# Norm statistics per batch and weight splitting per piece, inside the causal and the merged stage

## The chip, the cores and the metric

The kernel runs on one core of a Trainium2 chip. The metric is the device time of one execution in microseconds (us), the median of several runs. A core has a matmul engine (PE, its weight loads shown apart as PEld), a vector engine (DVE), an activation engine (ACT), a general engine (POOL) and a sync engine (SP) that here only issues DMAs. Each engine runs its own instructions in order, and the engines meet by semaphores.

## The reference, cut to what matters

Two layers follow each other on 16 batches of 256 rows with 256 features. The context has 77 rows per batch.

```
h = layernorm(x + multihead(x, x, x, sa_w..., causal=True))            # 16 heads of 16
h = layernorm(h + multihead(h, ctx, ctx, ca_w..., causal=False))
x = layernorm(h + relu(h @ ff_w1.T + b1) @ ff_w2.T + b2)              # hidden size 1024
q, k, v = x @ Wq + bq, ctx @ Wk + bk, ctx @ Wv + bv                    # second layer, one head
a = softmax(q k^T / 16) v
out = a * mask * sigmoid(concat(q, a) @ Wg + bg) + x

layernorm: std = sqrt(sum((x - mean)^2) / (d - 1));  gamma * (x - mean) / (std + 1e-6) + beta
```

## The kernel before, in words

Everything is fp32 accuracy made from products of two or three parts: a matrix is split in a high part (a rounded copy, made on ACT) and a low part (the rest, made on DVE or POOL), and three matmuls replace one (helper `mm3`, line 76).

The program is a row of stages. Between two stages all engines meet at a barrier (`Sems.stage`):

1. `context_products`: keys, values and folded weights that depend on the context alone, written to DRAM.
2. `self_attention`, here called the causal stage: causal attention, residual into `t.res` (all 16 batches stay in SBUF), and per 128 rows `bn_stats`/`bn_aggr` into `t.mv` (mean and variance).
3. `finish_stats`: for all 32 row groups at once `std = Sqrt(var)` on ACT, then `mean`, `rstd` on DVE.
4. `split_weights`: loads ca_wq, ca_wo, ff_w1, ff_w2 through two staging buffers and splits each in two.
5. `cross_feed_forward`, here called the merged stage: the first norm applied, cross attention, a second norm, feed-forward, statistics of the third.
6. `finish_stats` again.
7. `gated_attention`, the gated stage: third norm applied, second layer, output.

Stages 2 and 5 are software pipelines written out by hand. A list `slots` runs over pairs (n, s). The causal stage has U = 12 slots per n, the merged stage U = 8. Each engine walks the same list and does, in each slot, what its own loop says, for batches n-4 to n+4. So a batch is many slots under way, and in a steady batch period each engine does one batch's worth of every step. Names used later:

- Causal stage. PE: `scores_turned(g)` writes transposed scores to one of two buffers `a_st`, and waits for the exponential of two units before. `project_qk` (slots 3 to 6), `project_v` (slots 9, 10; it waits for `s_r1`). ACT: `exps(g)` one unit per slot (`a_pT<-a_st`), then in slot 7 `part_one` (`a_parts<-a_misc`). DVE: `remainder` (`a_rest`) makes `s_r1`. `moments` in slots 3 and 4.
- Merged stage. PE: one buffer `c_st` for transposed scores; `up_tile` and `down_tile` of the feed-forward, one each per slot. ACT per slot: `exps`, `hidden_high` (`c_hh`). In slot 6 of every batch there is already a `deviation`: the standard deviation of the second norm as exp(0.5 ln(var)), two activations on 2 columns. DVE follows in slot 7 with `inverse`: reciprocal, times var, plus std, scale, reciprocal (one refinement step of the root), each waiting for the one before.
- `feed_residual`, `feed_moments`: residual and statistics for the third norm, for batch n-6 or n-7.
- SP in the merged stage, per batch in this order: `store_parts`, `load_keys` (6 DMAs), `load_values`, `load_queries` (3 DMAs, after the store has landed).
- First in the merged stage DVE clears two tiles `c_nm` and sets rows of three `c_sk` to one, and waits for all of them.

## Time and profile before

| | us |
|---|---|
| runs shown | 1029.33, 1028.06, 1033.78 |
| median | 1029.33 |
| profiled execution, its own time | 1023.21 |
| its span, first to last instruction | 1021.5 |
| PE busy | 835.2 (82%) |
| DVE busy | 634.9 (62%) |
| ACT busy | 481.3 (47%) |
| POOL busy | 465.0 (46%) |
| mean granted clock of PE | 0.895 of full |

Start and end of the stages in the profiled execution, read from the timeline: context stage to 80, causal stage to 422, statistics and weights to 443, merged stage to 898, statistics to 902, gated stage to the end. Busy time is summed over stages that have different limits. A row of the timeline gives start, duration, engine, line, output<-inputs, a count of merged instructions, and in brackets how long the engine had stood idle and what released it.

### The profile page before, as it was taken

How to read it: one execution, taken by the hardware profiler on the slowest of the kernel's cores; microseconds unless marked ns; L12 is line 12 of the kernel's file. 1: busy time of each engine (PE TensorE's matmuls, PEld its weight loads, DVE VectorE, ACT ScalarE, POOL GpSimd, SP SyncE). 2: the span in 40 equal slices, each digit the busy share in tenths (PEclk: the TensorE clock that was granted, in tenths of full speed). 3: DMA queues.
4: the chain of work that ended last, by engine and by line, in shares of the span. 5: the costliest groups of instructions: out<-in, count | busy, mean ns of one | idle time of the engine just before them, and what ended most of it. 6: DMA issues, size and time to landing. Idle time of an engine off the chain costs nothing. (4 is left out here: it accounts for less than half of the span.)

```text
span 1021.5 us, 19656 instructions
## 1 busy us (share of the span) xinstructions
PE 835.2 (82%) x7264; PEld 684.1 (67%) x7264; DVE 634.9 (62%) x1315; ACT 481.3 (47%) x953; POOL 465.0 (46%) x584
## 2 busy tenths in 40 slices
PE   5965689999999988215778999999988888949997
PEld 4654567777777755214455777878877778949996
DVE  2533466767767766344568777888766566525664
ACT  4411145455555546122556666666554555334542
POOL 3003347666566647111224555555544455643440
PEclk9986799999999999655667999999999999967988
DMA  7393888877877750116434322222321000022433
GB/s 230 136 347 83 196 172 176 166 143 166 163 160 150 144 104 3 60 44 150 101 78 100 89 63 64 65 64 64 69 66 41 1 2 1 2 84 71 124 110 100
DMA packets 71103, 105.99 MB, mean 104 GB/s; under 512 B 21656, under 2 KB 60698, under 8 KB 66142
## 3 DMA queue, kind: packets, MB, share of 16 engines
q1 hardware_dynamic: 67244, 98.46, 41.0%
q10 hardware_dynamic: 3764, 6.29, 1.7%
q8 instruction: 58, 0.95, 0.4%
q14 instruction: 37, 0.30, 0.1%
HBM read 68.57 MB, written 35.62 MB: 102 GB/s over the span
## 5 line engine op out<-in xcount | busy, mean ns | idle before, releaser
L1283 DVE TENSOR_REDUCE a_nm<-a_s 128x2 f32<-128x512 f32 (+1 forms) x192 | 129.2, 681 | 83.3 <-PE a_s L1107 81.4
L1249 ACT ACTIVATE a_pT<-a_st 128x512 f32<-128x512 f32 x192 | 111.7, 594 | 108.5 <-PE a_st L1130 107.1
L976 POOL TENSOR_TENSOR c_hl<-c_hid,c_hh 128x256 fp32r<-128x256 f32 x128 | 95.1, 743 | 146.2 <-DVE c_hid L866 145.5
L697 ACT ACTIVATE c_pT<-c_st 77x512 f32<-77x512 f32 x128 | 75.6, 591 | 141.1 <-PE c_st L570 131.8
L616 PE MATMUL c_down<-fw,c_hh 128*128 128x256 f32 x512 | 116.0, 295 | 0.0
L866 DVE TENSOR_SCALAR c_hid<-c_up,ff_b_col 128x256 f32<-128x256 f32 x128 | 61.5, 480 | 74.6 <-ACT c_hh L721 74.5
L76 PE MATMUL c_up<-c_fxh,fw 128*128 128x256 f32 x512 | 102.0, 292 | 2.4 <-DVE c_hid L866 2.4
L1392 POOL TENSOR_SCALAR_AFFINE_SELECT a_pT<-a_pT 128x256 f32<-128x256 f32 (+1 forms) x192 | 89.2, 482 | 27.7 <-ACT a_pT L1249 27.3
L616 PEld LDWEIGHTS c_down<-fw,c_hh 128*128 128x128 f32 x512 | 87.7, 192 | 14.4 <-issue 14.4
L1130 PE MATMUL a_st<-a_sq,a_sk 98*128 98x256 bf16 (+1 forms) x512 | 74.7, 249 | 16.6 <-DMA a_sq<-a_mT 12.0
L76 PEld LDWEIGHTS c_up<-c_fxh,fw 128*128 128x128 f32 x512 | 80.2, 193 | 3.9 <-DVE c_hid L866 3.4
L1107 PE MATMUL a_s<-a_sk,a_sq 96*128 96x256 bf16 (+1 forms) x512 | 76.2, 252 | 0.0
L721 ACT ACTIVATE c_hh<-c_up,ff_b_col 128x256 fp32r<-128x256 f32 x128 | 59.3, 464 | 34.1 <-PE c_up L76 34.1
L797 DVE TENSOR_REDUCE c_nm<-c_s 128x5 f32<-128x385 f32 (+1 forms) x96 | 55.1, 574 | 32.1 <-PE c_s L550 32.0
L76 PE MATMUL c_up<-c_fxl,fw 128*128 128x256 f32 x256 | 72.7, 284 | 0.0
L616 PE MATMUL c_down<-fw,c_hl 128*128 128x256 f32 x256 | 72.6, 283 | 0.0
L1105 PE MATMUL a_s<-maskb,identb 128*128 128x256 bf16 (+1 forms) x192 | 62.3, 324 | 8.3 <-DMA a_sk<-qk_parts 7.8
L550 PE MATMUL c_s<-c_sk,c_sq 96*128 96x77 bf16 x512 | 38.8, 214 | 25.3 <-DVE c_nm L797 14.6
L570 PE MATMUL c_st<-c_sq,c_sk 98*77 98x256 bf16 x256 | 55.1, 300 | 3.7 <-ACT c_pT L697 3.7
L1107 PEld LDWEIGHTS a_s<-a_sk,a_sq 96*128 96x128 bf16 x512 | 46.8, 102 | 12.0 <-issue 1.9
L1130 PEld LDWEIGHTS a_st<-a_sq,a_sk 98*128 98x128 bf16 x512 | 34.5, 98 | 27.8 <-DMA a_sq<-a_mT 11.3
L931 POOL TENSOR_TENSOR res<-c_z,ln_b 128x512 f32<-128x512 f32 x16 | 20.5, 1279 | 71.2 <-ACT c_z L649 71.2
(242 smaller groups left out, 2294.6 us busy)
## 6 DMA issues: line engine op xcount, KB each, us to landing
qk_parts<-a_parts SPq DMA_DIRECT2D x16, 768.0 KB
a_sq<-qk_parts SPq DMA_DIRECT2D x16, 384.0 KB, 5.3
a_sk<-qk_parts SPq DMA_DIRECT2D x16, 384.0 KB, 7.1
q_parts<-c_parts SPq DMA_DIRECT2D x16, 384.0 KB, 5.4
c_sq<-q_parts SPq DMA_DIRECT2D x16, 384.0 KB
g_vv<-vv_rows SPq DMA_DIRECT2D x16, 308.0 KB
vv_rows<-x_vv SPq DMA_DIRECT2D x9, 512.0 KB, 2.9
x<-in_xT SPq DMA_DIRECT2D x16, 256.0 KB, 9.3
```

The lines of the kernel that those rows point to most:

```text
L76: last = pe.matmul(out, a(x, kt), b(y, kt), start=start and n == 0, stop=stop and n == len(seq) - 1)
L616: last = mt(down[:, qt * D:(qt + 1) * D], (hh, hl)[x][:, m, qt * P:(qt + 1) * P], w2[y][:, m, :], start=m == 0 and qt == 0 and i == 0, sto ...
L697: nc.scalar.activation(pT[g % NPT][:], st_ps[0:SC, :], ACT.Exp).then_inc(s_exp, 1)
L721: nc.scalar.activation(hh[:, m, :], up[n % 2][:, 0:S], ACT.Relu, bias=b1[:, m:m + 1]).then_inc(s_hh, 1)
L866: nc.vector.tensor_scalar(hid[n % NHID][:], up[n % 2][:, 0:S], b1[:, m:m + 1], 0.0, ALU.add, ALU.max).then_inc(s_hid, 1)
L976: nc.gpsimd.tensor_tensor(hl[:, m, :], hid[n % NHID][:], f32(hh[:, m, :]), ALU.subtract).then_inc(s_hl, 1)
L1105: mt(diag, t.identb[:], t.maskb[:, 0:len(heads), :], start=True, stop=False, skip_group_check=True)
L1107: last = mt(out[:, i * w:(i + 1) * w], sq[c % NSTK][0:KS, h, qt * P:(qt + 1) * P], sk[c % NSTK][0:KS, h, 0:w], start=False, stop=True, ski ...
L1130: last = mt(st_ps[g % 2][:, i * w:(i + 1) * w], sk[c % NSTK][:, h, kt * P:(kt + 1) * P], sq[c % NSTK][:, h, q0:S], start=True, stop=True, ...
L1249: nc.scalar.activation(pT[g % NPT][:], st_ps[g % 2][:], ACT.Exp).then_inc(s_exp, 1)
L1283: nc.vector.tensor_reduce(nm[c % 2][:, QT * heads[0] + qt:QT * heads[-1] + qt + 1:QT], s_ps[g % 2][:].rearrange("p (h k) -> p h k", h=len( ...
L1392: nc.gpsimd.affine_select(out=v, in_=v, compare_op=ALU.is_ge, fill=0.0, base=0, pattern=[[0, len(heads)], [1, P]], channel_multiplier=-1). ...
```

## The change

- `finish_stats` is gone. In the causal stage each batch gets `variance` (DVE, slot 4), `deviation` (ACT, slot 6, Ln then Exp with scale 0.5) and `inverse` (DVE, slot 9, five steps). In the merged stage the third norm gets the same per batch: `feed_variance` (DVE, slot 2), `feed_deviation` (ACT, slot 4), `feed_inverse` (DVE, slot 6).
- `split_weights` is gone. ca_wq and ca_wo are loaded at the end of SP's list in the causal stage, and split by the first instructions of the merged stage. ff_w1 and ff_w2 are loaded in the merged stage, behind the keys and values of three batches, which SP now issues first; they are split in six pieces during n = 1 to 3.
- In the merged stage the ones in `c_sk` are set later (n = -4, slots 5 to 7), and PE waits for them at the first use.
- In the causal stage x of the first two batches is split ahead of the loop. In the context stage one product (`square(0, ...)`) comes first on PE, and its two inputs first on ACT's DMA queue.
- In the gated stage five loads go from SP's queue to ACT's, ahead of all ACT work, and PE waits for them at first use.

```diff
@@ -703,6 +693,20 @@
                 atleast(act, s_y, c)
                 nc.scalar.activation(oh[:], o[:], ACT.Copy).then_inc(s_oh, 1)
 
+            def weight_high(i):
+                src, w, (hi, lo), k, scale = pieces[i]
+                act.wait_ge(loaded[w], 16)
+                nc.scalar.activation(hi[:, k, :], src[:, k, :], ACT.Copy, scale=scale).then_inc(s_wh, 1)
+
+            def feed_deviation(c):
+                if not real(c):
+                    return
+                n = QT * c
+                act.wait_ge(s_fvar, c + 1)
+                nc.scalar.activation(t.std[:, n:n + QT], t.var[:, n:n + QT], ACT.Ln).then_inc(s_fln, 1)
+                act.wait_ge(s_fln, c + 1)
+                nc.scalar.activation(t.std[:, n:n + QT], t.std[:, n:n + QT], ACT.Exp, scale=0.5).then_inc(s_fstd, 1)
+
             def deviation(c):
                 if not real(c):
                     return
...
@@ -737,11 +741,17 @@
                     part_two(n + 2)
                 if s == 5:
                     x_high(n + 3)
+                if s == 4:
+                    feed_deviation(n - 7)
                 if s == 6:
                     deviation(n - 3)
                 if s == 7:
                     shift_high(n)
                     o_high(n - 2)
+                if n == -4 and s in (0, 5):
+                    weight_high(s // 5)
+                if 1 <= n < 4 and s in (2, 6):
+                    weight_high(2 * n + s // 4)
 
         @block.vector
...
+                nc.vector.tensor_scalar(t.var[:, n:n + QT], t.mv[:, n:n + QT, 1], D / (D - 1.0), TINY, ALU.mult, ALU.max).then_inc(s_fvar, 1)
+
+            def feed_inverse(c):
+
+                if not real(c):
+                    return
+                n = QT * c
+                sd, out = t.std[:, n:n + QT], t.rstd[:, n:n + QT]
+                dve.wait_ge(s_fstd, c + 1)
+                nc.vector.reciprocal(froot[:], sd).then_inc(s_finv, 1)
+                dve.wait_ge(s_finv, c + 1)
+                nc.vector.tensor_tensor(froot[:], froot[:], t.var[:, n:n + QT], ALU.mult).then_inc(s_fquot, 1)
+                dve.wait_ge(s_fquot, c + 1)
+                nc.vector.tensor_tensor(froot[:], froot[:], sd, ALU.add).then_inc(s_froot, 1)
+                dve.wait_ge(s_froot, c + 1)
+                nc.vector.tensor_scalar(out, froot[:], 0.5, EPS, ALU.mult, ALU.add).then_inc(s_feps, 1)
+                dve.wait_ge(s_feps, c + 1)
+                nc.vector.reciprocal(out, out).then_inc(s_frstd, 1)
 
             def variance(c):
                 if not real(c):
...
@@ -885,10 +924,8 @@
 
             fstat = sb("fstat", [P, 6], F32)
             for v in nm:
-                nc.vector.memset(v[:], 0.0).then_inc(made, 1)
-            for v in sk:
-                nc.vector.memset(v[KS:KX], 1.0).then_inc(made, 1)
-            dve.wait_ge(made, 2 + NSTK)
+                nc.vector.memset(v[:], 0.0).then_inc(nm_made, 1)
+            dve.wait_ge(nm_made, 2)
             for n, s in slots:
                 g = U * n + s
                 if s == 7:
@@ -907,6 +944,7 @@
                     remainder(n + 2)
                     turn_back(n - 2, 0)
                     feed_moments(n - 7, 1)
+                    feed_variance(n - 7)
                 if s == 3:
                     centred(n + 4)
                 if s == 4:
@@ -918,6 +956,13 @@
                     x_low(n + 3)
                 if s == 6:
                     turn_back(n - 2, 1)
+                    feed_inverse(n - 7)
+                if n == -4 and s in (4, 7):
+                    weight_low(s // 7)
+                if n == -4 and s >= 5:
+                    nc.vector.memset(sk[s - 5][KS:KX], 1.0).then_inc(sk_ones, 1)
+                if 1 <= n < 4 and s in (3, 7):
+                    weight_low(2 * n + s // 7)
                 if s == 7:
                     shift_low(n)
...
@@ -1087,6 +1132,8 @@
                     store_parts(n + 2)
                     load_stacks(n + 2)
                     sp.dma_start(t.res[:, QT * (n + 2):QT * (n + 2) + QT, :], x_dram[n + 2]).then_inc(res_loaded[n % 2], 16)
+            for w, src, done in t.next_weights:
+                sp.dma_start(w[:], src).then_inc(done, 16)
 
         @block.tensor
         def _(pe):
...
@@ -1255,6 +1302,17 @@
                 atleast(act, s_y, c)
                 nc.scalar.activation(oh[:], o[c % 2][:], ACT.Copy).then_inc(s_oh, 1)
 
+            def deviation(c):
+                if not real(c):
+                    return
+                n = QT * c
+                act.wait_ge(s_var, c + 1)
+                nc.scalar.activation(t.std[:, n:n + QT], t.var[:, n:n + QT], ACT.Ln).then_inc(s_ln, 1)
+                act.wait_ge(s_ln, c + 1)
+                nc.scalar.activation(t.std[:, n:n + QT], t.std[:, n:n + QT], ACT.Exp, scale=0.5).then_inc(s_std, 1)
+
+            x_high(0)
+            x_high(1)
             for n, s in slots:
                 if s == 2:
                     shift_high(n - 1)
@@ -1265,7 +1323,9 @@
                     shift_rows(n - 1)
                 if s == 7:
                     part_one(n + 2)
-                if s == 9:
+                if s == 6:
+                    deviation(n - 4)
+                if s == 9 and n >= -1:
                     x_high(n + 3)
                 if s == 11:
                     spread_v(n + 2)
...
                     row += n * DH
 
+            for c in range(NSTK):
+                load_keys(c)
+                load_values(c)
+            for w, src, done in zip(raw[2:], (w1_dram, w2_dram), loaded[2:]):
+                sp.dma_start(w[:], src.rearrange("(k p) c -> p k c", p=P)).then_inc(done, 16)
             for c in range(B):
                 store_parts(c)
-                load_keys(c)
-                load_values(c)
+                if c >= NSTK:
+                    load_keys(c)
+                    load_values(c)
                 load_queries(c)
 
         @block.tensor
...
@@ -1349,6 +1433,9 @@
                     moments(n - 4, 0)
                 if s == 4:
                     moments(n - 4, 1)
+                    variance(n - 4)
+                if s == 9:
+                    inverse(n - 4)
                 if s == 5:
                     turn_av(n - 2, 0)
                 if s == 7:
...
@@ -1574,6 +1645,11 @@
 
         @block.scalar
         def _(act):
+            act.dma_start(f32(wqg[:].rearrange("p x k c -> p (x k c)")), d.wqg).then_inc(w_loaded, 16)
+            act.dma_start(f32(cb[:].rearrange("o b x s -> o (b x s)")), d.cb).then_inc(w_loaded, 16)
+            for v in vv:
+                act.dma_start(f32(v[SC:SCE].rearrange("p x c -> p (x c)")), d.row).then_inc(row_loaded, 16)
+
             def normed(c):
                 if not real(c):
                     return
...
```

DVE's `variance` and `inverse` of the causal stage read like `feed_variance` and `feed_inverse`, with `s_agg` and `s_std`.

ACT in the causal stage, one batch in steady state, before. The names are: `a_pT<-a_st` the exponentials, `a_mT` the maxima's high part, `a_parts` the queries' and keys' first part, `a_xh` the high part of x.

```order
L1242 DMA a_sq<-a_mT 2x32x128
L1249 ACTIVATE a_pT<-a_st 128x512 x4
L1220 ACTIVATE a_parts<-a_misc 128x2x512
L1249 ACTIVATE a_pT<-a_st 128x512 x2
L1213 ACTIVATE a_xh<-x 128x512
L1249 ACTIVATE a_pT<-a_st 128x512 x2
```

and of the change:

```order
L1289 DMA a_sq<-a_mT 2x32x128
L1296 ACTIVATE a_pT<-a_st 128x512 x3
L1310 ACT_TABLE_LOAD
L1310 ACTIVATE std<-var 128x2
L1312 ACT_TABLE_LOAD
L1312 ACTIVATE std<-std 128x2
L1296 ACTIVATE a_pT<-a_st 128x512
L1267 ACTIVATE a_parts<-a_misc 128x2x512
L1296 ACTIVATE a_pT<-a_st 128x512 x2
L1260 ACTIVATE a_xh<-x 128x512
```

Between the third and the fourth exponential stand two table loads and two activations, ahead of `a_parts`.

ACT in the merged stage, one batch from slot 4 to slot 7, before (`c_pT<-c_st` the exponentials, `c_hh` the hidden layer's high part, `c_xh` the high part of h):

```order
L697 ACTIVATE c_pT<-c_st 77x512
L721 ACTIVATE c_hh<-c_up,ff_b_col 128x256
L657 ACTIVATE c_xh<-c_hy 128x512
L697 ACTIVATE c_pT<-c_st 77x512
L721 ACTIVATE c_hh<-c_up,ff_b_col 128x256
L711 ACT_TABLE_LOAD
L711 ACTIVATE c_std<-c_var 128x2
L713 ACT_TABLE_LOAD
L713 ACTIVATE c_std<-c_std 128x2
```

and of the change:

```order
L687 ACTIVATE c_pT<-c_st 77x512
L725 ACTIVATE c_hh<-c_up,ff_b_col 128x256
L706 ACT_TABLE_LOAD
L706 ACTIVATE std<-var 128x2
L708 ACT_TABLE_LOAD
L708 ACTIVATE std<-std 128x2
L687 ACTIVATE c_pT<-c_st 77x512
L725 ACTIVATE c_hh<-c_up,ff_b_col 128x256
L647 ACTIVATE c_xh<-c_hy 128x512
L687 ACTIVATE c_pT<-c_st 77x512
L725 ACTIVATE c_hh<-c_up,ff_b_col 128x256
```

There are now two such groups in a batch, with two exponentials, two `c_hh` and one `c_xh` between them.

DVE at the start of the merged stage, before (`c_z` is the first norm's product):

```order
L124 UNCONDITIONAL_BRANCH
L128 SCALAR_TENSOR_TENSOR cwq<-wstage,cwq 128x512
L128 SCALAR_TENSOR_TENSOR cwo<-wstage,cwo 128x512
L128 SCALAR_TENSOR_TENSOR fw<-wstage,fw 128x2048 x2
L110 UNCONDITIONAL_BRANCH
L746 UNCONDITIONAL_BRANCH
L888 MEMSET c_nm 128x128 x2
L890 MEMSET c_sk 2x1232 x3
L754 SCALAR_TENSOR_TENSOR c_z<-res,mean,ln_g 128x256 x4
L805 TENSOR_TENSOR c_xl<-c_hy,c_xh 128x512
L818 TENSOR_TENSOR c_rest<-c_qm,c_parts 128x512
```

and of the change:

```order
L927 MEMSET c_nm 128x128 x2
L764 SCALAR_TENSOR_TENSOR c_z<-res,mv,ln_g 128x256 x2
L779 SCALAR_TENSOR_TENSOR c_wq<-raw_ca_wq,c_wq 128x512
L963 MEMSET c_sk 2x1232 x2
L779 SCALAR_TENSOR_TENSOR c_wo<-raw_ca_wo,c_wo 128x512
L963 MEMSET c_sk 2x1232
L764 SCALAR_TENSOR_TENSOR c_z<-res,mv,ln_g 128x256 x2
L844 TENSOR_TENSOR c_xl<-c_hy,c_xh 128x512
```

The first `c_z` comes ahead of the ones in `c_sk`; two low parts of weights now stand in this stage.

## Rows read from the trace of the kernel before

**Rows 1.** stretch: us, busy PE, PEld, DVE, ACT, POOL; PE clock, DMA share, GB/s
```profile
130.00:390.00 260.00, 233.81 (x2581) 182.29 (x2580) 183.33 (x341) 132.80 (x235) 164.90 (x247) 0.99 0.74 150
...
560.00:850.00 290.00, 264.66 (x2415) 225.77 (x2407) 215.57 (x511) 171.62 (x348) 157.48 (x178) 0.97 0.24 53
```

**Rows 2.** timeline of DVE, causal to merged: start, us, instruction [idle <-releaser]
```profile
421.80 0.18 DVE L1335 BATCH_NORM_AGGREGATE mv<-a_stat 128x2 f32<-128x6 f32 x1
...
439.69 2.29 DVE L128 SCALAR_TENSOR_TENSOR fw<-wstage,fw 128x2048 fp32r<-128x2048 f32 x1 [0.62 <-ACT fw L122]
...
443.39 1.08 DVE L890 MEMSET c_sk<- 2x1232 bf16 x1 [0.31 <-issue]
...
447.09 0.88 DVE L754 SCALAR_TENSOR_TENSOR c_z<-res,mean,ln_g 128x256 f32<-128x256 f32 x2
```

**Rows 3.** timeline, the same stretch, DMA issues of SP
```profile
429.92 1.00 SPq L116 DMA_DIRECT2D wstage<-in_L_xattn_ff_w  x2
459.73 0.37 SPq L471 DMA_DIRECT2D q_parts<-c_parts  x1
```

**Rows 4.** timeline, the same stretch, ACT and its weight wait
```profile
437.75 1.91 ACT L122 ACTIVATE fw<-wstage 128x2048 fp32r<-128x2048 f32 x1 [1.00 <-DMA wstage<-in_L_xattn_ff_w]
```

**Rows 5.** timeline, same stretch, first projection and first scores on PE
```profile
452.89 0.80 PE L76 MATMUL c_qm<-c_xh,cwq 128*128 128x256 f32 x2 [1.41 <-DVE c_xl L805]
...
471.87 0.57 PE L550 MATMUL c_s<-c_sk,c_sq 96*128 96x77 bf16 x6 [3.84 <-DMA c_sq<-q_parts]
```

**Rows 6.** timeline, merged to gated stage, last statistics and first work
```profile
897.90 0.18 DVE L884 BATCH_NORM_AGGREGATE mv<-c_fstat 128x2 f32<-128x6 f32 x1
...
902.65 2.06 ACT L1583 ACTIVATE g_z<-res,g_nmr,rstd 128x256 f32<-128x256 f32 x4
902.70 0.83 SPq L1497 DMA_DIRECT2D g_vv<-bias_row  x3
```

**Rows 7.** groups of ACT instructions by line: one norm's Ln and Exp
```profile
L711 ACT ACT_TABLE_LOAD x16 | 20.5, 1283 | 0.3
L713 ACT ACT_TABLE_LOAD x16 | 20.5, 1283 | 0.3
...
L711 ACT ACTIVATE c_std<-c_var 128x2 f32<-128x2 f32 x16 | 3.3, 204 | 0.2
```

**Rows 8.** timeline of ACT in one causal batch, slots 6, 7
```profile
202.62 0.60 ACT L1249 ACTIVATE a_pT<-a_st 128x512 f32<-128x512 f32 x1 [1.57 <-PE a_st L1130]
203.90 0.60 ACT L1249 ACTIVATE a_pT<-a_st 128x512 f32<-128x512 f32 x1 [0.68 <-PE a_st L1130]
204.39 1.02 ACT L1220 ACTIVATE a_parts<-a_misc 128x1024 bf16<-128x1024 f32 x1
...
222.72 1.02 ACT L1220 ACTIVATE a_parts<-a_misc 128x1024 bf16<-128x1024 f32 x1
```

**Rows 9.** timeline of DVE and, behind it, PE in the same batch
```profile
205.44 1.22 DVE L1298 TENSOR_TENSOR a_rest<-a_misc,a_parts 128x1024 f32<-128x1024 f32 x1 [0.52 <-ACT a_parts L1220]
...
206.72 0.39 PE L76 MATMUL a_misc<-swv,a_xh 128*128 128x256 f32 x1 [0.20 <-DVE a_rest L1298]
```

**Rows 10.** who PE waited for in 130:390 (us in total, times, longest)
```profile
PE a_st L1130 <- DMA a_sq<-a_mT: 12.0, 9, 3.1
```

**Rows 11.** timeline of ACT in one merged batch, slots 5 and 6
```profile
676.04 0.59 ACT L697 ACTIVATE c_pT<-c_st 77x512 f32<-77x512 f32 x1 [1.32 <-PE c_st L570]
...
678.51 0.59 ACT L697 ACTIVATE c_pT<-c_st 77x512 f32<-77x512 f32 x1 [1.03 <-PE c_st L570]
...
679.48 1.28 ACT L711 ACT_TABLE_LOAD   x1
```

**Rows 12.** timeline of PE behind it, slot 0 of the next batch
```profile
684.31 0.47 PE L76 MATMUL c_qm<-c_xh,cwq 128*128 128x256 f32 x2 [0.87 <-DVE c_mT L824]
```

**Rows 13.** DVE's step on the root, ns min/median/max
```profile
L784 DVE TENSOR_TENSOR c_root<-c_root,c_std x16: 163/1205/1222, 530.2 to 864.9; 128x2 f32<-128x2 f32 x16
```

**Rows 14.** timeline of ACT in the merged stage's last batches
```profile
879.02 0.48 ACT L721 ACTIVATE c_hh<-c_up,ff_b_col 128x256 fp32r<-128x256 f32 x1 [0.94 <-PE c_up L76]
```

More of the change, by code:

```diff
@@ L447, in cross_feed_forward @@
     hh, hl = sb("hh", [P, FT, S], F32R), sb("hl", [P, FT, S], F32R)
+    wq, wo, w1, w2 = ([sb(f"{n}{i}", [P, kt, c], F32R) for i in range(2)] for n, kt, c in (("wq", KT, D), ("wo", KT, D), ("w1", KT, F), ("w2", FT, D)))
+    raw = raw + [sb("raw_w1", [P, KT, F], F32), sb("raw_w2", [P, FT, D], F32)]
+    loaded = t.weights_loaded + [sem("up_weights"), sem("down_weights")]
+    pieces = [(raw[0], 0, wq, slice(0, KT), SCALE), (raw[1], 1, wo, slice(0, KT), 1.0)]
+    pieces += [(raw[2], 2, w1, slice(k, k + 1), 1.0) for k in range(KT)] + [(raw[3], 3, w2, slice(k, k + 2), 1.0) for k in range(0, FT, 2)]
     s_ps, st_ps, av_ps, hy, qm, down = ps("s"), ps("st"), ps("av"), ps("hy"), ps("qm"), ps("down")
@@ L611, in down_tile @@
                 pe.wait_ge(s_hl, FT * c + m + 1)
+                if c == 0 and m == 0:
+                    pe.wait_ge(s_wl, len(pieces))
                 if m == 0:
@@ L1256, in o_high @@
                 nc.scalar.activation(oh[:], o[c % 2][:], ACT.Copy).then_inc(s_oh, 1)
+            def deviation(c):
+                if not real(c):
+                    return
+                n = QT * c
+                act.wait_ge(s_var, c + 1)
[4 more added lines that the diff above has]
+            x_high(1)
             for n, s in slots:
@@ L1335, in moments, with variance, inverse @@
                 nc.vector.bn_aggr(t.mv[:, n, :], stat[:]).then_inc(s_agg, 1)
+            def variance(c):
+                if not real(c):
+                    return
+                n = QT * c
+                dve.wait_ge(s_agg, QT * (c + 1))
+                nc.vector.tensor_scalar(t.var[:, n:n + QT], t.mv[:, n:n + QT, 1], D / (D - 1.0), TINY, ALU.mult, ALU.max).then_inc(s_var, 1)
+            def inverse(c):
+                if not real(c):
+                    return
+                n = QT * c
+                sd, out = t.std[:, n:n + QT], t.rstd[:, n:n + QT]
+                dve.wait_ge(s_std, c + 1)
+                nc.vector.reciprocal(root[:], sd).then_inc(s_inv, 1)
+                dve.wait_ge(s_inv, c + 1)
+                nc.vector.tensor_tensor(root[:], root[:], t.var[:, n:n + QT], ALU.mult).then_inc(s_quot, 1)
+                dve.wait_ge(s_quot, c + 1)
+                nc.vector.tensor_tensor(root[:], root[:], sd, ALU.add).then_inc(s_root, 1)
+                dve.wait_ge(s_root, c + 1)
+                nc.vector.tensor_scalar(out, root[:], 0.5, EPS, ALU.mult, ALU.add).then_inc(s_eps, 1)
+                dve.wait_ge(s_eps, c + 1)
+                nc.vector.reciprocal(out, out).then_inc(s_rstd, 1)
             for v in nm:
@@ L1524, in scores @@
                     return
+                if c == 0:
+                    pe.wait_ge(w_loaded, 16 * 2)
+                    pe.wait_ge(s_one, 1)
                 pe.wait_ge(s_xl, c + 1)
@@ L1733, in program @@
         d.cb = nc.dram_tensor("key_bias", (1, B * 2 * SCE), F32).ap()
-        def weights(ctx, names, kts, colsn):
-            jobs, out_ = [], []
-            for (name, ap, scale), kt, c in zip(names, kts, colsn):
-                w = [sb(f"{name}{i}", [P, kt, c], F32R, ctx) for i in range(2)]
-                jobs.append((ap, w[0][:], w[1][:], scale))
-                out_.append(w)
-            with ExitStack() as st:
-                run(split_weights, st, sem, jobs)
-            return out_
```

133 lines of the change are left out of this document (55 added, 78 removed).

## The prediction

> **What bounds the kernel now.** I read the stretches first: who is busy where. In the steady part of the causal stage PE works 233.81 of 260 us, in that of the merged stage 264.66 of 290 us, and ACT only 51% and 59% [rows 1]. So PE sets the time there, with little room (2 us of idle time per batch of 18 to 23 us), and what counts of any added work is whether PE ends up waiting for it. Second I read the timeline between the stages [rows 2 to 6]: there PE has nothing to do, and every microsecond of hand-over is on the path. Third, the ACT rows in which the new work would stand [rows 7, 8, 11, 14], and PE's waits [rows 10, 12].
>
> **The gain: the hand-over to the merged stage.** Before, the last statistics end at 421.98, the last weight split at 441.98, then come three settings of ones (1.08 each), and the first norm product starts at 447.09 [rows 2]. After, behind 421.98 stand one variance (about 0.3), Ln and Exp with their table loads (2 x (1.283 + 0.204) = 2.97 [rows 7]), five small DVE steps (about 1.5; one of them takes 0.16 to 1.22 [rows 13]), one barrier (about 1.0) and the clearing of c_nm (0.3): the first product starts at about 428.3, 18.8 us earlier. On DVE, two splits of 0.7 and three settings of 1.3 with their gaps then lie between it and the first c_xl, where before nothing of that kind lay: they fill the time in which POOL, PE and ACT do their part, and run over by about 2 us. The first projection comes 16.8 us earlier than 452.89 [rows 5]. Next the store of the first parts and the queries' return: 459.73 to 471.87 before, 12.14 us [rows 3, 5]. Here 2 MB of feed-forward weights are ahead of it on the queues. Before, their issue at 429.92 and the start of the second split at 437.75 are 7.8 us apart [rows 3, 4]; that is how long they hold the queues. SP issues 18 key loads and 3 value loads first (13 us in all by before's pace of 4.35 us per batch), so weights end some 20 us after the stage began and the store comes at about 15 us. It can be held by 0 to 4 us. I take 1.5: **-15.5 us** for this hand-over (between -18 and -12).
>
> Weight pieces: six splits in n = 1 to 3, 3.8 us on ACT and 4.6 us on DVE by the durations of the two large splits (1.91 and 2.29 each [rows 4, 2]). PE waits for query DMAs there (3.84 us at its first [rows 5]), so part is hidden: **+2** (0 to 4.6).
>
> **The hand-over to the gated stage.** Before: last statistics end at 898.08, first g_z at 902.65 [rows 6], 4.6 us with one table load, four small steps and two barriers. After: 0.3 + 2.97 + 1.3 + one barrier of 0.9 = 5.5 us, and then ACT issues five DMAs before its first activation; SP needs 0.83 for three of them [rows 6], so about 1.6 to 2.4 on ACT. Together **+3** (+1 to +4). Nothing hides it, PE is idle until h is there.
>
> Context stage and causal start: one product of about 1.8 us goes into time in which PE waits for its first inputs, and x of the second batch is split early, behind which other waits come: **-1.5** (-3 to 0).
>
> **The price in the causal stage.** Each batch gets 2.97 us on ACT between the exponential of slot 6 and that of slot 7. In the batch shown, slot 6's starts at 202.62 and takes 0.60, then ACT is idle 0.68 to 203.90, and part_one starts at 204.39 [rows 8]. After: the block runs 203.22 to 206.19, the exponential takes 0.49 until part_one may start, part_one at 206.68 instead of 204.39, 2.29 later; DVE's remainder (1.22) and project_v follow directly: before, project_v at 206.72 had already waited 0.20 for this remainder [rows 9]. So PE stands 2.2 to 2.3 us longer before project_v, and what is behind it waits, since PE is in order. A part is absorbed, because PE had other waits in the same place: 12.0 us for the DMA of shifted rows in 260 us, some 14 batches of 18.3 [rows 10, 8], 0.86 each, of which this batch had 0.15. 2.27 - 0.71 = 1.55 us per batch. It falls on n = 4 to 13, where both the block and project_v exist: 10 x 1.55 = 15.5. In n = 14 to 17 only the two score buffers stand between ACT and PE, slots are shorter (1.1 us and less) and I take 2 each, 8. **+23.5 us**. Bounds: 0.7 x 14 = 10, if the 2.25 us of idle time before the two exponentials [rows 8] takes its full share, and 2.97 x 14 = 42, if nothing is absorbed. I take the middle since the wait of 0.20 shows that the chain is tight. The five DVE steps of slot 9 fall into DVE's own waits for scores: 0.
>
> **The price in the merged stage.** The same block stands in slot 4, two slots before the one that is there. ACT's idle time between the two places is 1.32 and 1.03 us [rows 11], 2.35 together; 2.97 - 2.35 = 0.62 us is left over. The old block starts at 679.48 directly behind, so it moves by that much, and behind it the maxima's high part, for which PE already waits 0.87 us [rows 12]: no slack there. DVE gets 5 steps (1.1 to 2.4 us, by the 0.16 and 1.22 of [rows 13]) ahead of feed_residual, in a stretch where it waits for ACT anyway: +0.3. So 0.9 x 12 (n = 7 to 18) = 11. In n = 19 to 21 only the feed-forward runs; ACT is busy 0.48 and idle 0.94 us per hidden part [rows 14]; the block is covered by two such gaps: 2.97 - 1.88 = 1.1 each, 3.3. **+14 us** (0, if DMA and DVE waits swallow all; 15 x 2.97 = 45, if none is covered).
>
> One rule bears on the size of the block. Each Ln and each Exp of before has a table load of 1283 ns [rows 7], 32 for 16 norms, and both instructions follow it at once. The Trainium skill ("ScalarE: Activation LUTs", "Table sets: the hidden batching unit") says that one set holds exp and ln and that the pair needs one load. By that rule with the set kept, no batch would load a table and the block would be 0.4 us; see rival 3. The page's section "What ACT_TABLE_LOAD costs" also gives 2.66 us per switch with a drain. The trace shows no drain: 32 loads with 0.6 us of idle time before them in all. By that figure a pair would be 5.7 us and the two stages would lose some 60 us more; the trace decides for 2.97.
>
> On the DVE step of 0.16 to 1.22 us: the Trainium skill ("SBUF — State Buffer", the section on engine ports) says that DVE with two SBUF inputs and POOL lock one port pair against each other. The trace agrees: median 1205 ns, 163 ns at the least, for 2 columns [rows 13]. Without the lock the DVE term would be nought instead of 0.3 per batch.
>
> **Sum**, against the profiled execution of 1023.2: -15.5 + 2 + 3 - 1.5 + 23.5 + 14 = +25.5, 1048.7 us. The median of the runs is 1029.3, 6 us above that execution; I add the difference to the median: **1055 us**.
>
> **Rivals.**
> 1. The blocks on ACT are hidden. Mechanism: in the causal stage part_one's delay is taken up by the DMA wait and the score buffers, in the merged stage by the 2.35 us of idle time and by DVE's waits. For it: ACT is idle half of the time [rows 1], DMA waits reach 3.1 us [rows 10]. Against it: project_v already waits for the remainder [rows 9], and PE for c_mT [rows 12]. What is left are the hand-overs, -15.5 + 2 + 3 - 1.5 = -12: 1017 us, faster. It decides if the causal price is under 0.9 us per batch with none in the merged stage.
> 2. Half of it: the causal price at its low bound, 10, and 3 in the merged stage: +1, 1030 us, no change.
> 3. The tables are not loaded again (the page's rule above): blocks of 0.4 us, 1017 us. Against it: the instruction order of the change has two loads in each of the 32 new blocks.
> 4. The merged stage is hit harder: two blocks within three slots, 5.9 us on ACT, hold both the single score buffer and the two buffers of the hidden layer, and DVE's five steps delay feed_residual, for which down_tile waits. 2.5 us in each of 15 batches, 38 instead of 14: 1079 us.
>
> **How the numbers follow.** A change within 0.5% (5 us, 1024 to 1034) can't be told from none. Forecast 0.67, rival 4 0.15, rival 1 0.08, rival 2 0.08, rival 3 0.02. Rivals 1 and 3 are faster, rival 2 is no change. The forecast's own range is 1040 to 1070 (causal 15 to 31, merged 8 to 22). The low end of the range takes in the upper edge of rival 2, the high end rival 4: 1033 to 1080. Faster 0.10, same 0.08, slower 0.82.
>
> **What would show it.** In the profile after: 97 table loads on ACT, those of the causal stage 32; part_one about 2.3 us later behind the exponential before it, and a PE wait for a_rest of 1.5 to 2.5 us in the steady batches; the causal period 18.3 us grown by 1.5; the merged period grown by about 1; the first projection of the merged stage some 17 us after the hand-over began to shorten, its first norm product about 6 us behind the last statistics; ACT's first activation in the gated stage behind five DMA issues. The prediction is wrong if the causal period has not grown, or if the merged one has grown by more than 2 us.

## The result, and the profile after

The changed kernel takes 1075.32 us (median of 4 runs, 1074.60 to 1078.71); the kernel before, in runs beside it, 1028.87 (1028.06 to 1033.78). The ratio is 1.045, 95% interval 1.041 to 1.049: slower by 46 us, where 25.5 were forecast. The profiled execution took 1075.48 us with a span of 1073.7, 52.2 more than before's. That is 6 us more than the medians differ, since before's profiled execution was 6 us faster than its median; so single rows below can be some us too large. The difference is made up as follows, read from the starts of the same instructions in both traces:

| part | forecast | measured | from |
| --- | --- | --- | --- |
| context stage and causal start | -1.5 | 0 | first a_parts at 87.17 and 87.13 |
| causal stage | +23.5 | +47.6 | last statistics 421.80 and 469.43 |
| hand-over to merged | -18.8, then the ramp | -20.7 | first c_z 447.09 and 474.03 |
| merged stage, first c_z to last statistics | +3.3 for the ramp, +2 pieces, +14 blocks | +20.8 | 897.90 and 945.65 |
| hand-over to gated, up to the first g_z | +3 | +1.9 | 902.65 and 952.25 |

(The ramp's 3.3 is what the forecast's 15.5 is short of 18.8. The gated stage holds the rest, 2.6 us. In the trace of run 12, whose gated stage is before's, it takes 3.3 us longer than in before's trace, so this rest can be scatter.)

The stretches of after that answer to [rows 1], and one of the steady part alone (columns: start:end, us, busy time of each engine, PE clock, DMA share, GB/s):

```profile
130.00:390.00 260.00, 221.41 (x2250) 172.57 (x2250) 181.68 (x344) 142.66 (x243) 145.28 (x213) 0.93 0.68 140
190.00:390.00 200.00, 169.42 (x1701) 132.75 (x1702) 144.16 (x279) 111.92 (x191) 111.16 (x163) 0.91 0.64 132
560.00:850.00 290.00, 263.31 (x2361) 217.48 (x2362) 233.65 (x560) 197.37 (x384) 149.36 (x166) 0.94 0.28 61
```

The same steady stretch of before:

```profile
190.00:390.00 200.00, 181.42 (x2014) 141.06 (x2013) 143.18 (x273) 102.01 (x182) 128.43 (x194) 0.99 0.70 143
```

Two things are to be seen. PE gets through 16% fewer matmuls in the same 200 us, and each takes longer (0.100 us of busy time per matmul, 0.090 before), while its granted clock is 0.91 and not 0.99. One causal batch (a_parts of c = 6 to c = 15) lasts 22.19 us and not 18.60. Over just these nine batches, after and then before, with PE's busy time alone:

```profile
190.05:389.78 199.73, 169.42 (x1701) 0.91 0.64 132
185.70:353.10 167.40, 153.60 (x1706) 1.00 0.76 157
```

PE is busy 18.8 us a batch, where it was busy 17.1 for the same work: 1.8 us of the 3.6 are slower matmuls. The other 1.8 are idle time (3.4 and 1.5 a batch). PE's waits in 190:390, in all, times, longest, first of after and then of before:

```profile
PE a_misc L76 <- DVE a_rest L1358: 10.3, 8, 1.4
PE a_misc L76 <- DVE a_mT L1351: 7.2, 9, 1.0
PE a_st L1177 <- DMA a_sq<-a_mT: 6.6, 4, 2.2
PE a_st L1177 <- ACT a_pT L1296: 6.2, 5, 1.2
```

```profile
PE a_st L1130 <- DMA a_sq<-a_mT: 8.0, 7, 3.1
PE a_misc L76 <- DVE a_mT L1291: 6.5, 9, 0.7
PE a_misc L76 <- DVE a_rest L1298: 2.0, 5, 0.5
PE a_st L1130 <- ACT a_pT L1249: 1.4, 2, 0.7
```

Together 30.3 us in 9.0 batches against 17.9 in 10.8. One batch shows how both come about. ACT's timeline of after, the place of [rows 8] (start, us, instruction, idle before it):

```profile
231.06 0.60 ACT L1296 ACTIVATE a_pT<-a_st 128x512 f32<-128x512 f32 x1 [1.57 <-PE a_st L1177]
231.68 1.28 ACT L1310 ACT_TABLE_LOAD   x1
...
234.60 0.58 ACT L1296 ACTIVATE a_pT<-a_st 128x512 f32<-128x512 f32 x1
235.08 1.02 ACT L1267 ACTIVATE a_parts<-a_misc 128x1024 bf16<-128x1024 f32 x1
```

From that exponential to part_one it is 4.02 us, where it was 1.77: 2.25 later, as worked out (2.29). DVE (with one row of POOL) and PE behind it:

```profile
236.12 1.22 DVE L1358 TENSOR_TENSOR a_rest<-a_misc,a_parts 128x1024 f32<-128x1024 f32 x1 [2.76 <-ACT a_parts L1267]
...
239.00 2.13 POOL L1469 TENSOR_TENSOR a_parts<-a_rest,a_parts 128x1024 bf16<-128x1024 f32 x1
239.17 1.98 DVE L1415 TENSOR_TENSOR a_root<-a_root,std 128x2 f32<-128x2 f32 x1
```

```profile
231.11 0.48 PE L76 MATMUL a_misc<-a_xh,swk 128*128 128x256 f32 x2
...
235.32 0.39 PE L1177 MATMUL a_st<-a_sq,a_sk 98*128 98x256 bf16 x2 [1.24 <-DMA a_sq<-a_mT]
...
237.40 0.58 PE L76 MATMUL a_misc<-swv,a_xh 128*128 128x256 f32 x1 [1.36 <-DVE a_rest L1358]
...
240.37 0.63 PE L76 MATMUL a_misc<-swo,a_oh 128*128 128x256 f32 x2
...
244.67 0.40 PE L76 MATMUL a_misc<-swo,a_oh 128*128 128x256 f32 x2
```

PE stands for 1.24 and 1.36 us within 4 us, and then the same pair of matmuls of 256 columns takes 0.63 us until it takes 0.40 again. The stretches of this batch say it by the clock (busy time is PE's alone, the clock is the column behind it):

```profile
233.00:237.00 4.00, 1.79 (x24) 0.97 0.37 105
237.00:241.00 4.00, 3.60 (x16) 0.50 0.00 0
241.00:245.00 4.00, 4.00 (x36) 0.68 0.55 197
245.00:249.00 4.00, 3.99 (x50) 1.00 0.84 158
```

0.50 is the lower of its two levels (1.2 of 2.4 GHz). It fell behind the 4 us in which PE was busy 1.79, and for about 6 us each matmul took longer. Not every batch has it. Four batches in a row, c = 10 to 13, from a_parts to a_parts:

```profile
280.56:301.49 20.93, 17.32 (x189) 1.00 0.63 129
301.49:322.42 20.93, 17.30 (x189) 1.00 0.69 140
322.42:344.52 22.10, 18.78 (x189) 0.92 0.70 147
344.52:367.76 23.24, 19.88 (x189) 0.85 0.59 120
```

At full clock a batch still lasts 20.9 us, 2.3 more than before's 18.6. So the block costs 2.3 us a batch without any change of the clock, and what the lower clock adds, on the mean of the nine batches, is 1.3. (The busy time grows by more than that; the idle time in front of other steps shrinks a little when PE is slower.) Gaps of this length do not always bring the clock down: the second of the four batches has them too and stays at 1.00. (Its first gap is put down to ACT's exponential, which stands behind the block; the one of the same length above, at 235.32, to a DMA that landed at about that time.)

```profile
301.73 0.38 PE L1177 MATMUL a_st<-a_sq,a_sk 98*128 98x256 bf16 x2 [1.24 <-ACT a_pT L1296]
303.81 0.39 PE L76 MATMUL a_misc<-swv,a_xh 128*128 128x256 f32 x1 [1.37 <-DVE a_rest L1358]
```

The table loads are 97 on ACT, as forecast: 16 in each of the six lines of the per-batch norms (the causal one shown) and one in the gated stage.

```profile
L1310 ACT ACT_TABLE_LOAD x16 | 20.5, 1283 | 0.3
L1312 ACT ACT_TABLE_LOAD x16 | 20.5, 1283 | 0.3
```

The hand-over to the merged stage, after's timeline where [rows 2] is before's:

```profile
466.60 1.28 ACT L1310 ACT_TABLE_LOAD   x1
...
469.43 0.18 DVE L1395 BATCH_NORM_AGGREGATE mv<-a_stat 128x2 f32<-128x6 f32 x1
469.64 0.17 DVE L1402 TENSOR_SCALAR var<-mv 128x2 f32<-128x2 f32 x1
469.85 0.20 ACT L1310 ACTIVATE std<-var 128x2 f32<-128x2 f32 x1 [1.96 <-DVE var L1402]
470.07 1.28 ACT L1312 ACT_TABLE_LOAD   x1
...
474.03 0.88 DVE L764 SCALAR_TENSOR_TENSOR c_z<-res,mv,ln_g 128x256 f32<-128x256 f32 x2
```

Ln's own table load is not on this path: ACT did it at 466.60, 3 us before the variance was there, while it had nothing else, and Ln follows the variance at 0.04 us. Only Exp's load lies between. That makes the first c_z 4.6 us behind the last statistics, not 6.3. The first projection's and the first scores' waits, the place of [rows 5]:

```profile
481.98 0.77 PE L76 MATMUL c_qm<-c_xh,c_wq 128*128 128x256 f32 x2 [3.62 <-DVE c_xl L844]
...
503.43 0.57 PE L531 MATMUL c_s<-c_sk,c_sq 96*128 96x77 bf16 x6 [6.35 <-DMA c_sq<-q_parts]
```

The projection comes 7.95 us behind the first c_z (5.80 before), the scores 29.40 (24.78 before): 2.1 for DVE's splits and ones, as forecast (2), and 2.5 more for the queries.

### The profile page after: what moved, and what is told of

Its sections match the earlier page's. It is cut to its first block and busy times, and to the rows that moved or that the text cites. A ratio compares the mean times of both kernels' runs of the same rounds, so it can differ in the third digit from the quotient of the medians.

```text
span 1073.7 us, 19902 instructions
## 1 busy us (share of the span) xinstructions
PE 868.4 (81%) x7264; PEld 704.0 (66%) x7264; DVE 699.0 (65%) x1505; ACT 565.9 (53%) x1079; POOL 466.7 (43%) x584
## 5 line engine op out<-in xcount | busy, mean ns | idle before, releaser
L1021 POOL TENSOR_TENSOR c_hl<-c_hid,c_hh 128x256 fp32r<-128x256 f32 x128 | 95.1, 744 | 158.7 <-DVE c_hid L905 158.0
L607 PE MATMUL c_down<-c_w,c_hh 128*128 128x256 f32 x512 | 118.9, 300 | 6.8 <-DVE res L913 6.8
L76 PE MATMUL c_up<-c_fxh,c_w 128*128 128x256 f32 x512 | 103.3, 295 | 1.5 <-DVE c_hid L905 1.5
L607 PEld LDWEIGHTS c_down<-c_w,c_hh 128*128 128x128 f32 x512 | 89.6, 196 | 22.1 <-issue 18.2
L1177 PE MATMUL a_st<-a_sq,a_sk 98*128 98x256 bf16 (+1 forms) x512 | 79.2, 261 | 26.2 <-ACT a_pT L1296 15.3
L76 PEld LDWEIGHTS c_up<-c_fxh,c_w 128*128 128x128 f32 x512 | 81.6, 197 | 3.2 <-DVE c_hid L905 2.6
L1154 PE MATMUL a_s<-a_sk,a_sq 96*128 96x256 bf16 (+1 forms) x512 | 78.6, 258 | 0.0
L607 PE MATMUL c_down<-c_w,c_hl 128*128 128x256 f32 x256 | 73.7, 288 | 0.0
L76 PE MATMUL c_up<-c_fxl,c_w 128*128 128x256 f32 x256 | 73.5, 287 | 0.0
L76 PE MATMUL a_misc<-swv,a_xh 128*128 128x256 f32 x128 | 37.6, 355 | 18.2 <-DVE a_rest L1358 18.2
```

The lines of the kernel that those rows point to most:

```text
L76: last = pe.matmul(out, a(x, kt), b(y, kt), start=start and n == 0, stop=stop and n == len(seq) - 1)
L607: last = mt(down[:, qt * D:(qt + 1) * D], (hh, hl)[x][:, m, qt * P:(qt + 1) * P], w2[y][:, m, :], start=m == 0 and qt == 0 and i == 0, sto ...
L1021: nc.gpsimd.tensor_tensor(hl[:, m, :], hid[n % NHID][:], f32(hh[:, m, :]), ALU.subtract).then_inc(s_hl, 1)
L1154: last = mt(out[:, i * w:(i + 1) * w], sq[c % NSTK][0:KS, h, qt * P:(qt + 1) * P], sk[c % NSTK][0:KS, h, 0:w], start=False, stop=True, ski ...
L1177: last = mt(st_ps[g % 2][:, i * w:(i + 1) * w], sk[c % NSTK][:, h, kt * P:(kt + 1) * P], sq[c % NSTK][:, h, q0:S], start=True, stop=True, ...
```

## The experiments

Twelve kernels ran; each ratio is against the kernel before in runs beside it. The medians of before in these were 1028.3 (runs 1 to 4), 1030.0 (5 to 8) and 1028.1 (9 to 12), so a difference between runs of two such groups can be off by 2 us from this alone. Theory A says that the block of Ln, Exp and two table loads ahead of part_one sets the causal loss, by PE's waits and by the clock that they bring down.

**1. Causal norm once.** `deviation`, `variance` and `inverse` are taken out of the causal loops:

```
-                if s == 6:
-                    deviation(n - 4)
...
+            deviation(0)        # behind the loop, over columns 0:NT; variance, inverse likewise
```

> The changed kernel, but in the causal stage variance, Ln, Exp and the five DVE steps run once over all 32 columns behind the last batch, not per batch. Theory A (the block of Ln, Exp and two table loads on ACT, 2.97 us ahead of part_one in every batch, makes PE wait, and the waiting lowers PE's granted clock): the causal stage gives back what it lost, about 45 us, 1075 becomes 1030; PE's clock in the steady stretch is back at 0.99 or 1.00 and its waits for a_rest fall from 10.3 us to about 1.5. Theory B (the DVE steps do it): 1030 too, so this run does not part A from B. Theory C (it is neither; the weight loads and the early x_high have shifted the stage): 1070 or more.

1030.99 us, ratio 1.004 (1.001 to 1.007). The clock in 190:390 is 0.99, PE's waits for a_rest 1.6 us in all, a batch 18.49 us. Theory C falls: in the trace the stage, from its first a_parts to its last statistics, takes 336.7 us (382.3 in the changed kernel, 334.6 before), so all but 2 us of its loss are the norm's.

**2. Copies for Ln and Exp.**

```
-                nc.scalar.activation(t.std[...], t.var[...], ACT.Ln).then_inc(s_ln, 1)
+                nc.scalar.activation(t.std[...], t.var[...], ACT.Copy).then_inc(s_ln, 1)
...
-                nc.scalar.activation(t.std[...], t.std[...], ACT.Exp, scale=0.5).then_inc(s_std, 1)
+                nc.scalar.activation(t.std[...], t.std[...], ACT.Copy, scale=0.5).then_inc(s_std, 1)
```

> The changed kernel, but in the causal stage Ln and Exp of each batch are two Copy activations on the same tiles: no table loads there, every instruction, wait and DVE step stays (the first norm is computed from the wrong root). The block on ACT is 0.4 us instead of 2.97. Theory A (the table loads): 1035, and PE's clock back at 0.99 to 1.00. Theory B (the five DVE steps in slot 9 hold back the maxima, and so the scores): at most 10 us less than 1075, 1065 or more.

1033.18 us, ratio 1.006 (1.003 to 1.010). Of the 44 us that run 1 gives back, the loads alone hold 42; both activations, their waits and all DVE steps are still there. A batch lasts 19.0 us, clock 1.00. The 0.5 us a batch above run 1 are what the short activations and DVE's steps cost without the loads.

**3. DVE's steps late.** The loop's `inverse(n - 4)` goes, one `inverse(0)` over 32 columns stands behind it.

> The changed kernel, but the five DVE steps of the causal stage are done once over 32 columns behind the last batch; variance, Ln, Exp and the table loads stay in every batch. Theory A: 1067 to 1075, the causal period stays at 22 us. Theory B (DVE steps): 1035, period back at 18.7 us.

1075.56 us, ratio 1.048 (1.039 to 1.057), a batch 22.20 us. Theory B falls: sixteen times five DVE steps, one of them about 2 us long in ten of the batches, cost nothing that can be measured in the whole. The four times spread over 15 us (1070.62 to 1085.49), so the batch's length says more than the median. One trace of a difference there is: this run's two full-clock batches last 20.6 us, the changed kernel's 20.9, so DVE's steps hold such a batch up by 0.4 us, which the mean over all batches does not show.

```profile
347.78:368.34 20.56, 17.26 (x189) 1.00 0.62 133
```

**4. Merged norm once.** As 1, for `feed_variance`, `feed_deviation`, `feed_inverse`.

> The changed kernel, but in the merged stage the norm after the feed-forward gets variance, Ln, Exp and the DVE steps once behind the last batch. Theory A (the second block in each batch holds up the feed-forward, 0.34 us per steady batch and 7.8 in the last four batches; the 7 us in the first four batches belong to the weight pieces): 1075 becomes 1063. Rival D (all of the merged stage's growth of 21 us comes from the weight pieces and the ramp): 1075, no change. Rival E (all of it is the block's): 1054.

1068.82 us, ratio 1.039 (1.032 to 1.046), beside 1.045 of the changed kernel, whose interval it overlaps. Its profile is clearer: first c_z to last statistics takes 459.0 us, 471.6 in the changed kernel, 450.8 before. So 12.6 of the 20.8 are the blocks', and D and E are both out. (The median falls by only 6.5: in this trace the causal stage, the same code as in the changed kernel, took 7.2 us longer, 389.5 against 382.3.) The run takes out ACT's loads and DVE's steps together; which of the two costs the 12.6 was not parted.

**5. Half as many blocks.**

```
-                if not real(c):
+                if not real(c) or c % 2 == 0:
...
-                n = QT * c
+                n = QT * (c - 1)     # four columns instead of two, in deviation and inverse
```

> The changed kernel, but in the causal stage the block of Ln, Exp and the DVE steps comes at every second batch, for the four columns of two batches: half as many blocks, each with its two table loads. Theory A with a price per block that does not depend on the others (44 us for 16 blocks by the run that took them all out, 2.8 each): eight blocks give back 22, 1053. If a block is partly absorbed when the batch before it left PE ahead: below 1045. If the lower clock is a matter of any block at all: above 1060, and the clock in the stretch still at 0.91 or less.

1057.35 us, ratio 1.027 (1.022 to 1.032); the middle forecast, 1053, lies just below the interval's 1053.1 to 1062.9 (ratio times 1029.99). The price per block is about the same (by the ratios 3.0 us, against 2.6 with sixteen blocks), if anything above it. The clock is 0.97, between the 0.91 with all blocks and the 0.99 with none.

**6. The block behind part_one.**

```
-                if s == 6:
+                if s == 8:
                     deviation(n - 4)
...
-                if s == 9:
+                if s == 11:
                     inverse(n - 4)
```

> The changed kernel, but the causal block of ACT stands in slot 8, behind part_one and the exponential of that slot (the DVE steps in slot 11). Theory A1 (the path is part_one, the remainder on DVE, project_v on PE): PE's wait for a_rest falls back to 2 us or less, and the stage gives back more than half, 1050 or less. Theory A2 (any 3 us on ACT cost the same, since the exponentials stand in one row and PE follows them with two buffers): 1070 to 1075, with the waits now at the scores (a_st for ACT's exponentials).

1045.74 us, ratio 1.019 (1.013 to 1.024): A1. The waits for a_rest are 2.0 us in all, the clock 0.97, a batch 19.7 us. The same 3 us on ACT cost 15 us two slots later and 44 where they were. PE now waits 5.2 us for DVE's maxima, as it had not before.

**7. More work for PE.**

```
                 if kt_ == 0:
+                    g = U * (c - 2) + 9 - ST_LAG
+                    if real(g // U):
+                        atleast(pe, s_exp, g - 1)
+                        for _ in range(6):
+                            mt(st_ps[g % 2][:, 0:512], t.identb[:], ..., start=True, stop=True, ...)
                     pe.wait_ge(s_r1, c + 1)
```

> The changed kernel, but in front of each project_v whose scores buffer exists, where PE waits for a_rest, it does six more bf16 matmuls of 512 columns (about 1.3 us, into a scores buffer that the next scores overwrite). Theory F (some 15 us of the causal stage's loss is a lower granted clock, which comes of PE's idle time in front of project_v): the clock in the steady stretch rises from 0.91 towards 0.99 and the time falls by 5 to 15 us, to 1060 to 1070, although PE has more to do. Rival G (the clock has nothing to do with these gaps, or the work is simply added): 1075 or up to 12 us more.

1075.41 us, ratio 1.046 (1.041 to 1.052): by the time, rival G. By the trace, half of each theory came out. The clock rose to 0.97, and the stretch got faster, not slower, though PE has more to do: a batch lasts 21.35 us and not 22.19. The stretch and the added line of this run (x instructions, busy us, mean ns, idle before):

```profile
190.00:390.00 200.00, 175.20 (x1790) 132.55 (x1787) 149.80 (x287) 115.48 (x196) 115.24 (x167) 0.97 0.65 132
```

```profile
L1227 PE MATMUL a_st<-maskb,identb 128*128 128x512 bf16 x60 | 16.8, 422 | 5.0 <-ACT a_pT L1304 4.8
```

In 9.4 batches (period 21.35) PE is busy 175.20 us, 16.8 of them with the filler: 16.9 per batch are left for the kernel's own work, about what it is before (17.1), and 1.9 less than in the changed kernel. Seven of the nine batches from c = 6 on have the full clock, where two had it, and last 21.0 us each, as the full-clock batches without the filler do (20.9). So the clock did follow the gaps, and the filler brings the time back only to what the block costs at full clock. In the trace the causal stage is 5.5 us shorter (376.8 against 382.3), the low end of theory F's 5 to 15. The median does not show it: its four times go from 1071.84 to 1082.90, and in the trace the merged stage, the same code, took 2.9 us longer.

**8. Both norms once.** The edits of 1 and 4 together.

> The changed kernel with both norms (the first and the one behind the feed-forward) taken once behind the last batch of their stage; weights are still split piece by piece and loaded early. If the parts add: 1031.0 of the causal part alone less 6.5 of the merged part alone = 1024.5, which is 4 us under the kernel before (0.996). If the merged block costs more once the causal stage is fast: 1018. If nothing of it is left: 1031.

1021.63 us, ratio 0.992 (0.990 to 0.995): 8 us under before. Against run 1 the merged blocks give 9.4 by the medians and 12.5 in the traces (472.8 and 460.3), as in run 4. What is left of the merged stage's growth is 9.5 us (460.3 against 450.8), and nearly all of it, 8.6, is there by the eighth c_xh (99.2 us behind the first, 90.6 before).

**9. Feed-forward weights behind the first queries.**

```
-            for w, src, done in zip(raw[2:], ...): sp.dma_start(...)   # ahead of the loop
...
                 load_queries(c)
+                if c == 0:
+                    for w, src, done in zip(raw[2:], ...): sp.dma_start(...)
```

> The version with both norms once (1021.6), but SP issues the feed-forward weights' loads behind the first batch's store and query loads, not ahead of them. Its ramp in the merged stage is 8.5 us longer than before's up to the eighth c_xh, of it 4.2 up to the first scores, where PE waits 6.0 us for the queries' DMA instead of 3.8. Theory Q (the 2 MB of weights hold the queues): first scores 2 us earlier, the stage 2 to 4 us shorter, 1018 to 1020. Rival W (the weight pieces and ones on DVE and ACT do it): no change, 1021 to 1022.

1017.84 us, ratio 0.991 (0.987 to 0.994). The intervals of 8 and 9 overlap, so the time alone does not tell; in the traces the first scores come 24.23 us behind the first c_z, 29.01 in run 8, PE's longest wait for the queries is 3.4 us, not 6.0, and the stage is 4.0 us shorter (456.3). Theory Q, with first scores 4.8 us earlier where 2 were forecast.

**10. One Sqrt for each norm.**

```
+                act.wait_ge(s_agg, NT)
+                nc.scalar.activation(t.std[:], t.mv[:, :, 1], ACT.Sqrt, scale=D / (D - 1.0))
...
+                nc.vector.tensor_scalar(t.rstd[:], t.std[:], EPS, None, ALU.add)
+                nc.vector.reciprocal(t.rstd[:], t.rstd[:])
```

> The kernel of the run before it, but both norms' ends are made as the kernel before makes them: one Sqrt on ACT over 32 columns and two DVE steps, in place of variance, Ln, Exp and five DVE steps. Each hand-over loses one table load of 1.28 us, an activation and four small DVE steps with their gaps, 2 to 2.5 us: 4 to 5 us in all, 1014 to 1016.

1010.42 us, ratio 0.984 (0.980 to 0.987). Each hand-over is 2.6 us shorter (last statistics to first c_z 5.11 to 2.51, to first g_z 7.23 to 4.64), 5.2 in all, as expected; the medians are 7.4 apart, more than the traces explain. DVE's side of it:

```profile
428.10 0.18 DVE L1372 BATCH_NORM_AGGREGATE mv<-a_stat 128x2 f32<-128x6 f32 x1
428.58 0.18 DVE L1383 TENSOR_SCALAR rstd<-std 128x32 f32<-128x32 f32 x1 [0.30 <-ACT std L1290]
...
430.61 0.48 DVE L759 SCALAR_TENSOR_TENSOR c_z<-res,mv,ln_g 128x256 f32<-128x256 f32 x1
```

Sqrt with its wait lies in 0.30 us: its table was there already.

**11. Splits and ones later.** The split of the output projection and the ones go from n = -4 to n = -1.

> The kernel of the run before it, but the output projection's split and the three settings of ones come in n = -1 of the merged stage, where PE waits for the queries, not in n = -4. Rival W of the load order's run: first parts at 8.8 us behind the first norm product, not 10.9, and 2 us off the time, 1012 to 1014. If DVE is not what the first parts wait for: no change.

1010.52 us, ratio 0.983 (0.980 to 0.986): no change. The first parts do come at 8.78 us, not 10.88, but the stage takes 455.2 us as in run 10. The 2.1 us were gained at that place and are lost again within the next batches.

**12. The causal block alone.** The kernel before, with `variance`, `deviation` and `inverse` in its causal stage as in the changed kernel, and nothing else.

> The kernel before with one part of the change alone: variance, Ln, Exp and the five DVE steps per batch in the causal stage, at the changed kernel's places (the own stage behind it stays, and overwrites their result). Theory A: the causal stage grows by 44 to 47 us as in the changed kernel, 1028 becomes 1073, with PE's clock in the steady stretch at about 0.91. If the block costs that much only beside the early loads and the early splits of x: 1050 or less.

1079.34 us, ratio 1.051 (1.047 to 1.055). Its causal stage ends at 470.16, 48.4 us later than before's; a batch is 21.95 us. Its stretch:

```profile
190.00:390.00 200.00, 167.71 (x1708) 131.17 (x1708) 145.56 (x281) 113.72 (x192) 111.78 (x164) 0.93 0.66 132
```

The block needs nothing else of the change to cost what it costs.

## Why the prediction was right, and where its size was off

The direction and the mechanism were right, and the sum was 21 us short. That 1075.3 lies in the range, 1033 to 1080, is in part luck: the forecast's own range ended at 1070, and the part above it was there for rival 4, which puts the added loss in the merged stage. The loss came in the causal stage.

- **Causal stage, 23.5 forecast, 47.6 measured: the mis-sized term.** The first step held: part_one came 2.25 us later. Two steps behind it did not. "2.27 - 0.71 = 1.55" let PE's other waits absorb a part, but the batches at full clock are 2.3 us longer than before's, in this trace as in run 12 (20.9 us), and 2.0 longer without DVE's steps (run 3, 20.6): at most 0.3 of 2.25 was absorbed. The sign named for it, a wait for a_rest of 1.5 to 2.5 us, did not show either (1.4 at the most), since part of the delay already falls in front of the scores (1.24). And "10 x 1.55 = 15.5" took waits as the whole price, at an unchanged PE; the lower clock adds 1.3 a batch. The true number is 3.6 a batch; over the 9 from c = 6 to 15 that is 32. Up to c = 6 the stage had lost 4.4, and the rest of 47.6, 11, came behind c = 15, where 8 were forecast. My high bound, 2.97 x 14 = 42, was no bound: a delay of 2.97 can cost more than 2.97 when the engine behind it slows down (batch c = 13 lasts 23.2 us, 4.6 more than before's mean).
- **DVE's steps of slot 9, 0 forecast:** right in the mean by run 3 (22.20 us a batch without them, 22.19 with them), short by 0.4 in a full-clock batch. The step of 1.98 us is longer than any in [rows 13]. The prediction cited the Trainium skill ("SBUF — State Buffer", engine ports) for such a length; the trace agrees, for the long step ends as POOL's a_parts (239.00, 2.13 us) does.
- **Tables, rival 3:** out. The Trainium skill ("ScalarE: Activation LUTs", "Table sets: the hidden batching unit") says that ln and exp can share one load. In this trace each block has two, and run 2, the block without them, prices them at 42 us in the causal stage: that is what the rule, with its set kept from batch to batch, would have saved.
- **Hand-over to the merged stage, -15.5 forecast with its ramp:** the first c_z gained 20.7, not 18.8, by the table load that ran ahead. But first scores lost 4.6 of it, not 3.3, so the term came out at -16.1. The risk named there, 0 to 4 us for the weights on the queues, shows as 2.5 against before; run 9 shows that the weights hold the queries by 4.8. Without them the way from the first projection to the first scores is 16.3 us, shorter than before's 19.0, and this gain, which the forecast did not have, hid the difference.
- **Merged stage, +16 forecast.** 20.8 less the 4.6 up to the first scores leaves 16.2. Its parts are not where I put them. The blocks cost 12.6 (run 4) for 14 forecast, but in the steady part only 0.34 a batch, not 0.9 (from the first to the thirteenth c_fxh, the high part of the feed-forward's input: 277.35 and 281.40 us), and most of it behind that, where soon nothing but the feed-forward is left: 81.1 us to the last statistics, 71.6 before, 72.2 in run 8. The down-projection's waits, for the residual that DVE adds, are 6.8 us in all, four times 1.5 to 2.0 in the last four batches, and nought before and in run 4:

```profile
L607 PE MATMUL c_down<-c_w,c_hh 128*128 128x256 f32 x512 | 118.9, 300 | 6.8 <-DVE res L913 6.8
```

  That is the second mechanism of rival 4, at 6.8 us and not at 2.5 in each of 15 batches. The weight pieces, +2 (0 to 4.6), were not run alone. In run 10, with the blocks and the weights' hold on the queues gone, the stage still takes 4.4 us longer than before (455.2), and by the eighth c_xh it is 4.5 us late (95.1 against 90.6): if that is theirs, they cost about twice the forecast.
- **Hand-over to the gated stage, +3 forecast, +1.9 measured:** again Ln's table was loaded ahead.
- **Context stage, -1.5 forecast, 0 measured:** the causal stage starts at the same time in both traces.

What the rest of the change is worth shows in runs 8 and 10. With both norms taken once, and the weights split and loaded inside the stages, it is 0.8% under the kernel before (1021.6 us); with the feed-forward weights' loads behind the first queries and one Sqrt for each norm besides, 1.6% (1010.4 us). Not settled is why the medians of runs 9 and 10 are 7.4 us apart and the traces 5.2. That the clock fell because of the two gaps, and not of some other property of the stretch, rests on run 7 alone, which fills one of them; why batches with the same two gaps (c = 10 and 11) kept the full clock is open.

## What to carry to other kernels

Work that swaps an activation table belongs where it happens once, behind the last batch, not in a loop whose other activations need another table; what counted here is not the instruction (0.2 us) but its load (1.28). If it must stand in the loop, put it behind the operation that TensorE waits for, not ahead: the same 3 us cost a third two slots later. When an added delay makes a nearly full TensorE wait, price the delay in full unless a trace shows what absorbs it (2.0 of 2.25 us came through here), and add a term for the clock (1.3 here).

## What was not expected of the hardware

- Two waits of PE of 1.24 and 1.36 us within 4 us were followed by some 6 us at clock 0.50, in which a pair of matmuls took 1.6 times as long (0.63 for 0.40 us). Two other batches with such gaps stayed at 1.00. In before, with waits of up to 3.1 us [rows 10], the same stretch has 0.99.
- Six more matmuls of 512 columns per batch, 16.8 us of work in 200, cost no time that could be measured (1075.41 and 1075.32), and in the trace a batch was 0.8 us shorter with them.
- The table load of an activation that waits for a semaphore runs before the wait is over: where ACT is idle, as at the stages' ends, it costs nothing.
- The same DVE step on 128x2 took 1.98 us in the batch shown, beside a POOL instruction of 2.13 us, and 0.16 behind the last one (at 471.99), with POOL idle.
